# The closing chunk of an attention layer: four PSUM banks for the sums, half weighings between single additions

## The reference

```
xl = (x @ Wl).reshape(-1, H, C);  xr = (x @ Wr).reshape(-1, H, C)
e = leaky_relu(xl[src] + xr[dst], 0.2)
logits = einsum('ehc,hc->eh', e, att)
m = segment_max(logits, dst, num_segments=N_NODES)
p = exp(logits - m[dst])
denom = segment_sum(p, dst, num_segments=N_NODES)
alpha = p / denom[dst]
out = segment_sum(alpha[:, :, None] * xl[src], dst, num_segments=N_NODES)
return out.mean(axis=1) + bias
```

## Time and profile before

| | us |
|---|---|
| median of 3 runs | 7916.43 |
| lowest and highest | 7906.61, 7916.87 |
| the profiled execution | 7905.31 |
| its span | 7903.6 |
| busy PE, DVE, ACT, POOL | 6022.1, 3735.6, 1755.1, 3860.4 |

### The profile page before, as it was taken

The page is one execution under the profiler, slowest core; times in us unless marked ns, Lnnn a source line. Parts: engine busy times, 40 slices in busy tenths (PEclk is TensorE's granted clock), DMA queues, the critical chain, the costliest instruction groups (busy, mean ns, idle before and its releaser), DMA issues.

```text
span 7903.6 us, 136433 instructions
## 1 busy us (share of the span) xinstructions
PE 6022.1 (76%) x46669; PEld 3947.9 (50%) x46669; DVE 3735.6 (47%) x7081; ACT 1755.1 (22%) x3748; POOL 3860.4 (49%) x4028
## 2 busy tenths in 40 slices
PE   5888886666666777678777876778877758788877
PEld 4666665566655666534444443344444434444444
DVE  5444443555564555534444445444444544444445
ACT  2222221333330000022222221222222222222221
POOL 4555553444435455355555542555555345555551
PEclk8888886777777777788898897888888978898888
DMA  4444442222212222233333332333333323333332
GB/s 101 130 130 129 128 129 84 54 58 57 58 53 59 61 59 62 55 75 91 89 91 88 93 84 54 85 90 91 91 87 86 83 53 90 89 91 92 89 89 62
DMA packets 689768, 660.52 MB, mean 84 GB/s; under 512 B 398899, under 2 KB 481274, under 8 KB 689082
## 3 DMA queue, kind: packets, MB, share of 16 engines
q1 hardware_dynamic: 555754, 484.41, 20.5%
q0 software_dynamic: 128960, 166.69, 11.1%
q10 hardware_dynamic: 4368, 0.70, 0.1%
HBM read 562.14 MB, written 89.17 MB: 82 GB/s over the span
## 4 chain that ended last, share of the span: by engine, by line
PE 50%; issue 20%; another core or an unknown queue 19%; DVE 6%; ACT 3%; DVEq 1%; DMA 1%; POOL 0%; ACTq 0%; POOLq 0%
PE ps L1050 13%; PE ps L895 12%; PE ps L989 6%; PE ps L910 2%; PE ps L850 2%; PE ps L1010 2%; PE ps L1000 2%; PE ps L975 1%; PE ps L859 1%; DVE region L1773 1%; PE ps L969 1%; DVE acc L1783 1%; PE ps L837 1%; ACT region L657 1%
## 5 line engine op out<-in xcount | busy, mean ns | idle before, releaser
L376 POOL DMA_INDIRECT rows<-table,idx x2340 | 2254.7, 964 | 2258.1 <-ACT region L646 967.9
L1050 PE MATMUL ps<-region,hot 128*128 128x272 f32 x4992 | 1534.1, 458 | 281.5 <-DVE region L1751 152.6
L1050 PEld LDWEIGHTS ps<-region,hot 128*128 128x128 f32 x4992 | 1040.7, 219 | 679.1 <-issue 423.0
L895 PE MATMUL ps<-hot,region 128*128 128x192 bf16 (+1 forms) x8640 | 1116.6, 291 | 322.5 <-issue 293.5
L1783 DVE TENSOR_TENSOR acc<-acc,ps 128x272 f32 x1248 | 544.9, 437 | 1705.0 <-remote 772.8
L657 ACT ACTIVATE region<-ps 128x512 f32<-128x512 f32 x1248 | 677.4, 595 | 2689.7 <-remote 1434.7
L895 PEld LDWEIGHTS ps<-hot,region 128*128 128x128 bf16 x8640 | 910.6, 116 | 463.7 <-issue 390.3
L363 POOL DMA_INDIRECT rows<-table,idx x728 | 697.5, 958 | 531.5 <-PE ps L830 317.3
L989 PE MATMUL ps<-xT,wcat 64*128 64x512 f32 x2496 | 770.7, 695 | 218.5 <-issue 108.4
L1773 DVE TENSOR_TENSOR region<-ps,region 128x1056 f32<-128x1056 f32 x624 | 777.7, 1252 | 50.5 <-issue 46.1
L393 POOL DMA_INDIRECT rows<-table,idx x480 | 456.9, 952 | 503.5 <-PE ps L922 347.2
(11 more groups left out here) (303 smaller groups left out, 6769.0 us busy)
## 6 DMA issues: line engine op xcount, KB each, us to landing
hot<-hot_dram SPq DMA_DIRECT2D x624, 256.0 KB
turned<-turned_dram SPq DMA_DIRECT2D x624, 128.0 KB
rows<-table,idx POOLq DMA_INDIRECT x3548
hot_dram<-hot SPq DMA_DIRECT2D x104, 512.0 KB
region<-hot_dram SPq DMA_DIRECT2D x90, 512.0 KB
xwin<-table SPq DMA_DIRECT2D x1664, 24.0 KB
region<-d_dram SPq DMA_DIRECT2D x104, 256.0 KB
turned_dram<-turned SPq DMA_DIRECT2D x104, 256.0 KB
```

The costliest lines, as they stand in the source:

```text
L376: pool.indirect_dma_start(rows[:, n % 2, j, :], None, table, bass.IndirectOffsetOnAxis(ap=idx[:, s:s + 1], axis=0)).then_inc(rows_in3[n % ...
L895: mm = pe.matmul(ps[:, GB + i % 2, 224 * j:224 * j + n], bt[b][:, k, at:at + P], tabparts[:, k::FOLD, (2 + s) * C:(3 + s) * C], start=(k = ...
L1050: mm = pe.matmul(ps[:, AG + i, 0:PC + H], hot[:, b, 4 * side + 2 * i + j, :], px[b][:, 4 * side + 2 * i + j, :], start=(j == 0), stop=(j = ...
```

## The change

`TAIL` is 96, the first group of the closing chunk. From there on:

- Side 1's sums go to the banks `Z` and `Z + 1` (`sum_bank`), side 0's stay in `AG` and `AG + 1`. So a bank is used again after four sums, not two, and PE's wait is for the addition four sums back. In group 96, side 1 waits for no addition.
- `weigh_two(k, side, i)` weighs two slots, 528 elements a lane. Only the second of a side signals `px_made`.
- DVE's order in a step is: a half weighing of group k + 1, one addition of group k, four times over. In step 113 only the additions are left.
- Groups below 96 keep their order. `add` now calls `add_one` twice.

```diff
+TAIL = G - 8
+        def sum_bank(k, side, i):
+            return Z + i if k >= TAIL and side == 1 else AG + i
@@ sums_half
-                    of_bank = 4 * (l * G + k) + 2 * side + i - 1
-                    if of_bank > 0:
+                    of_bank = 4 * (l * G + k) + 2 * side + i - (3 if k > TAIL else 1)
+                    if of_bank > 0 and not (k == TAIL and side == 1):
                         pe.wait_ge(att_added, of_bank)
...
-                        mm = pe.matmul(ps[:, AG + i, 0:PC + H], hot[:, b, 4 * side + 2 * i + j, :],
+                        mm = pe.matmul(ps[:, sum_bank(k, side, i), 0:PC + H], hot[:, b, 4 * side + 2 * i + j, :],
@@ attention
+                def weigh_two(k, side, i):
+                    n, j = piece_of(k), 4 * side + 2 * i
+                    if i == 0:
+                        v.wait_ge(xs_kept, l * G + k + 1)
+                        if k % 2 == 1:
+                            v.wait_ge(one_kept, (l * G + k) // 2 + 1)
+                    to = px[k % 2][:, j:j + 2, 0:PC].rearrange("p j (h k) -> p j h k", k=HK)
+                    at = ps[:, PB, :].rearrange("p (j a r) -> p a j r", j=4, a=2)[:, side, 2 * i:2 * i + 2, H * n:H * n + H]
+                    made = v.tensor_tensor(to, at.unsqueeze(3).broadcast_to([P, 2, H, HK]),
+                                           xs[:, (k // 8) % 2, k % 8, j:j + 2, :].unsqueeze(2).broadcast_to([P, 2, H, HK]),
+                                           ALU.mult)
+                    if i == 1:
+                        made.then_inc(px_made, 1)
+                def add_one(k, side, i, windows):
+                    m = 4 * (l * G + k) + 2 * side + i
+                    at = acc[:, bass.ds(windows[2 * side + i], 1), 0:PC + H].rearrange("p a c -> p (a c)")
+                    v.wait_ge(att_summed, m + 1)
+                    v.wait_ge(att_added, m)
+                    v.tensor_tensor(at, at, ps[:, sum_bank(k, side, i), 0:PC + H], ALU.add).then_inc(att_added, 1)
@@ the steps' loop
+                    elif k >= TAIL:
+                        for side in range(2):
+                            for i in range(2):
+                                if k + 1 < G:
+                                    weigh_two(k + 1, side, i)
+                                add_one(k, side, i, windows)
```

## The result

| | before | changed |
|---|---|---|
| median of 5 runs, us | 7906.61 | 7872.5 |
| lowest and highest | 7881.39, 7916.87 | 7852.71, 7890.42 |
| the profiled execution | 7905.31 | 7890.42 |
| its span | 7903.6 | 7888.7 |
| the three tails, summed | 120.98 | 94.81 |

The ratio of the changed kernel to the one before is 0.9964, with a 95% interval of 0.9946 to 0.9981: 28.5 us faster, between 15 and 43 (the two medians lie 34.1 us apart). The forecast was 22.3 us faster, and the tails of the traces give 26.2. So the kernel went the forecast way by about the forecast amount, and the level was wrong.

What follows compares the result with a forecast made beforehand. VectorE was taken to set the tail's pace, with TensorE waiting for it. Six groups of 4.24 us plus 7.46 make 32.9 a layer, 22.3 us gained in all: 7894 us, with 8 in 10 for 7880 to 7909.

Steps and rivals of the forecast that it cites:

- the level: Whole program's forecast time: 7894 us, from a median of 7916.4 less 22.3.
- the pause: VectorE idle 0.36 us before each pair's second addition, for the previous addition's end and address building; would go.
- the cover: Half weighing between additions: next addition starts 0.54 us after the last one's end, hiding 0.36 with 0.18 spare.
- The steady group: Groups 97 to 101 of each layer: period 4.24 us instead of 4.97, 0.73 gained each.
- the edge: From a group's last addition to the next group's first weighing, where a table entry is read: 0.69 us.
- The first group: Group 96: side 1 runs at once in free banks; 4.24 us instead of 6.03, 1.79 gained.
- The end: Groups 102 and 103: additions become the bound; 7.46 us instead of 8.84, 1.38 gained.
- The sum: Three layers' tails: 32.9 us each, gains of 6.9, 7.6 and 7.8, together 22.3 us.
- No overlap between VectorE instructions: Rival: 0.08 us overlaps missing beside half weighings, 4.87 us a group, 7906 us in all; chance 0.09.
- The address work uncovered: Rival: each addition comes 0.36 us after its weighing's end, 6.0 us a group, 7931 us; chance 0.04.
- The one-hot copies: Rival: copies of one-hot matrices set the period if latency exceeds 4.46 us; at 5.0, 7899 us; chance 0.05.
- The clock in the tail: Rival: granted clock 0.50 for a stretch makes TensorE the bound, 1 to 3 us a layer, 7897 to 7903; chance 0.07.

Runs made afterwards that it cites:

- banks alone: Kernel before with side 1's sums in two further banks, VectorE's old order kept; ratio 0.9976, tails 114.30 us.
- paired: Changed kernel with two half weighings, then two additions, per side, as in the old grouping; ratio 0.9998, tails 117.21 us.
- the copy on the fourth chip: Kernel before, unedited, run as a kernel of its own; ratio 0.9992, tails 119.73 us.
- read ahead: Changed kernel with the next group's table entry read before a group's third addition; ratios 0.9943 and 0.9962, tails 91.21 us.
- the order alone: Changed kernel with only two banks for the sums, half weighings and single additions kept; ratio 0.9981, tails 105.16 us.
- group 96 held: Changed kernel with side 1 of group 96 in the two old banks, waiting for additions; one execution, no ratio, tails 100.59 us.

## Why the prediction was right and wrong

**What bounds the tail, and the pause: right.** VectorE set the pace (banks alone: period 5.0), and the pause behind an addition was what the order removes (paired: it is back). That the pause is a wait and an address together holds with 0.09 and 0.27 us. The size of the cover was right too: the address rows run under the half weighing.

**The steady group: 4.05 us, forecast 4.24.** The half weighing was right (0.70 for 0.705, its successor 0.62 for 0.625 later). The term that was mis-sized is the edge. I took 0.69 us from rows in which the last addition stands behind its own pause; it is 0.49 or 0.56 now. The table entry's rows stand behind the address rows of that addition, and once these run under a half weighing the entry is read earlier too: in the trace of before TENSOR_LOAD starts 0.02 us behind the last addition's start (4765.95 and 4765.92), in the changed one 0.14 us ahead of it (4774.53 and 4774.67). Read an instruction earlier still, it costs nothing at all. That was 0.17 a group, nearly 1.0 us a layer.

**The first group: right, its reason in part.** 4.20 us in the first layer and 4.00 in the others, forecast 4.24, and the clock stayed up. Held back, it costs 2.0 us a layer, forecast 1.79. The prediction put the loss down to TensorE's idle stretch and the slow clock together; in the copy on the fourth chip the same idle stretch at full clock left 4.94 us. Of the 6.03 us some 1.1 are thus the clock, and the rest of the gain is the pauses of a steady group.

**The end: 7.08 us, forecast 7.46.** From the last addition of group 102 to the first of group 103 it is 0.73 us, not 1.1: the same edge term. The prediction added the table's load to the pause between two additions, and the load ran beside it: read ahead, the same distance is 0.71.

**The sum: 26.2 us, forecast 22.3.** Most of the 3.9 us of difference is the edge: five times 0.17 and 0.37 at the end make 1.2 us a layer. Group 96 was 0.24 us shorter than forecast in two layers.

**The level: wrong, and the step that failed.** It is the last one of the sum: "The runs shown have their median 11 us higher, 7916.4, from which I take the same 22.3: 7894", with a spread of 10 us taken from three runs. The runs showed another base and a wider spread. Of the 21.5 us between forecast and median, 9.8 are the median of before, which two further executions moved from 7916.4 to 7906.6; 3.9 are the tails; 7.8 remain. The five executions of the kernel before have a standard deviation of 14.4 us and lie within 36 us, the changed kernel's five have 13.7 and lie within 38, and the range went 14 us down. An estimate from these deviations: a median of five strays by some 8 us, so the 7.8 can be scatter alone. Where they come from stays open, since of the changed kernel's five executions only the slowest, 7890.4 us, has a trace. The forecast's own range was also added up wrong: 7894 with 6 and 5 above it is 7905, not 7902.

One place where executions differ can be seen in code that no kernel here changes. In the last steps of the first message passing layer, near 1250 to 1300 us, the additions of one line (start, time, idle before), in the trace of the order alone:

```profile
1258.03 0.22 DVE L1502 TENSOR_TENSOR acc<-acc,ps 128x65 f32 x1 [2.03 <-PE ps L864]
...
1265.54 0.22 DVE L1502 TENSOR_TENSOR acc<-acc,ps 128x65 f32 x1 [3.54 <-PE ps L864]
```

and in that of the paired kernel, on the same chip:

```profile
1259.43 0.22 DVE L1502 TENSOR_TENSOR acc<-acc,ps 128x65 f32 x1 [6.91 <-PE ps L864]
...
1272.81 0.22 DVE L1502 TENSOR_TENSOR acc<-acc,ps 128x65 f32 x1 [7.30 <-PE ps L864]
```

A step takes 7.51 us in the one and 13.38 in the other. The windows (length, PE busy, granted clock, DMA share, GB/s) of the first:

```profile
1260.00:1270.00 10.00, 8.44 (x83) 1.00 0.25 97
```

and of the second:

```profile
1260.00:1270.00 10.00, 9.22 (x44) 0.50 0.21 80
```

The same matmuls run at 2.4 GHz in one execution and at 1.2 GHz in the other, and it stays so for the last three to four steps. From the last pick of this layer (line 1478) to the first product with `gmask` (line 1635) of the next it is 63 to 64 us in five traces (order alone, group 96 held, and three on the fourth chip) and 83 to 87 us in the nine others. That is 20 us decided in a place that the change does not reach, twice the spread that I allowed. Both traces of the first chip took the longer way (83.5 and 84.9 us), so it does not explain the difference between these two; whether the executions without a trace took it is not known. What turns it to one side or the other was not tried.

**Whether the change gains more than its tails: open.** Its three ratios, weighted by their intervals, give 0.9957 with some 0.0009 to either side, 34 us, 7 either way, and the tails 26.2. Its medians lie 34.1, 34.2 and 29.8 us below those of before. Behind the tails no trace shows a gain (2980.9 us on the fourth chip, 2979.0 for the copy of before). So 26 us are shown with their place, and the rest is at the edge of the scatter.

**The rivals.** No overlap between VectorE instructions: refuted, 0.08 us less than its duration passes from each half weighing to its addition. The Trainium skill's rule of reducing operations and not waits ("VectorE: DVE Perf Modes", Rules for kernel authors) fails here, where 14 more operations a layer removed waits. (The prediction said 4 x 7; 28 half weighings stand in for 14 full ones.) The prediction also left out a sentence of the same page: in The DRAIN you can't avoid, the Trainium skill adds that a next operation that is not held starts earlier. The overlap of 0.08 us is thus no disagreement with it. The address work uncovered: refuted. The one-hot copies: in the changed kernel's trace a burst ended 3.2 us after the sums before it, and the copies never set the period, not even at 3.85 us. The clock in the tail: it stayed at 1.00 in all three.

## What to carry to other kernels

Where one engine sets the pace and pauses between an instruction and the next that depends on it and on an address in a register, put a piece of other work between them, longer than the pause, even if that means splitting it; read the numbers that addresses need an instruction earlier still. Banks or buffers help little while the engine that frees them is the bound: in the steady groups two more gave nothing in the old order, and about 0.2 us a group in the new one. Forecast a change of 0.3% as a difference to runs of the same chip, and give the level the whole spread of single executions, chips included.

## What the hardware showed beyond expectation

- The clock's granted level can differ between executions in the same code: at 0.50 for some 40 us with TensorE busy 9.2 of 10 us, or at 1.00 with 8.4 of 10. Behind an idle stretch of TensorE it fell to 0.50 in one trace (3.30 us idle) and stayed at 1.00 in another (3.29 us).
- A wait of VectorE for its own last instruction leaves it idle for 0.09 us and costs 0.18 from start to start; building an address from registers costs 0.26 more where nothing covers it. Covered by a half weighing both cost nothing.
- The same program took a median of 7777, 7779, 7891 and 7907 us on four chips, while its tails, in the three traces there are, agreed to 1.3 us in sum, and those of the changed kernel, on three chips, to 0.1 us.
